# First weight loads of a GNN and mixture-of-experts layer: up matrices of experts 0 to 2 in two transfers in place of three, asked for at other moments

## What is computed

```python
q, k, v = x @ wq.T, x @ wk.T, x @ wv.T                # 1024 x 1024 float32 each
q2, k2, v2 = q @ wiq.T, k @ wik.T, v @ wiv.T
gnn = softmax(q2 k2' / 8 + mask) v2 @ wo.T            # by head
mix = ln(h + attn(h @ mq, h @ mk, h @ mv) @ mo)       # linear attention
...
xe = (x1_norm * score_e)                              # rows scaled by the gate's score of expert e
h = square(relu(bf16(xe) @ bf16(w_up[e]).T))          # w_up: 8 x 1408 x 1024, given in float32
routed += bf16(h) @ bf16(w_down[e]).T                 # w_down: 8 x 1024 x 1408, given in float32
shared = square(relu(x1_norm @ shared_up.T)) @ shared_down.T   # float32
```

## Time and profile before

| what | us |
|---|---|
| median of 3 runs | 359.33 |
| the 3 runs | 359.3, 361.91, 359.33 |
| the profiled execution: its time | 357.42 |
| the profiled execution: its span | 356.1 |
| PE busy in the span | 307.5 |
| DVE, ACT, POOL busy | 111.4, 59.0, 34.2 |

### The profile page before, as it was taken

How to read it: one execution, slowest core, us unless ns; L and a number is a source line. 1 busy time by engine, 2 the same in 40 slices (tenths; PEclk the granted TensorE clock), 3 DMA queues, 4 the chain that set the end, 5 groups by cost and what they waited for, 6 DMA issues and landing times.

```text
span 356.1 us, 3105 instructions
## 1 busy us (share of the span) xinstructions
PE 307.5 (86%) x1236; PEld 149.9 (42%) x1236; DVE 111.4 (31%) x246; ACT 59.0 (17%) x113; POOL 34.2 (10%) x62
## 2 busy tenths in 40 slices
PE   4999998998999999999959998899998893473674
PEld 4344444333343343433324565543455661241343
DVE  6619436400143439200732312210222330101112
ACT  1410000010003010300020033300223440111131
POOL 0511010110110110211110001000000040000000
PEclk9999999999999999999989999999999996876889
DMA  7999999999999999999999999999999999999997
GB/s 296 387 356 311 395 342 309 353 347 320 431 309 377 393 276 429 265 420 329 307 367 309 211 431 336 218 223 210 225 212 213 225 209 225 213 213 212 209 215 157
DMA packets 8968, 104.90 MB, mean 295 GB/s; under 512 B 1120, under 2 KB 1592, under 8 KB 2812
## 3 DMA queue, kind: packets, MB, share of 16 engines
q0 software_dynamic: 7776, 97.52, 95.0%
q1 hardware_dynamic: 880, 7.05, 5.0%
q10 hardware_dynamic: 300, 0.16, 0.2%
HBM read 150.48 MB, written 0.39 MB: 424 GB/s over the span
## 4 chain that ended last, share of the span: by engine, by line
PE 66%; DMA 26%; DVE 3%; ACT 2%; issue 1%; another core or an unknown queue 1%
PE bank L844 32%; DMA stage<-in_expert_up 14%; PE bank L997 9%; PE bank L1018 9%; PE bank L978 6%; PE bank L1058 5%; DMA ring<-in_mat_wik 4%; DMA ring<-in_mat_mv 4%; DMA ring<-in_mat_wo 4%; PE bank L968 1%; PE bank L815 1%; ACT hbuf L451 1%; PE bank L852 1%; ACT xn L445 1%
## 5 line engine op out<-in xcount | busy, mean ns | idle before, releaser
L844 PE MATMUL bank<-ring,xnt 128*96 128x512 f32 x224 | 99.4, 600 | 0.9 <-ACT xnt L381 0.6
L844 PEld LDWEIGHTS bank<-ring,xnt 128*96 128x96 f32 x224 | 36.3, 165 | 58.8 <-issue 57.7
L1018 PE MATMUL bank<-stage,hbuf 128*96 128x512 bf16 (+5 forms) x242 | 44.0, 341 | 18.1 <-DMA stage<-in_expert_down 14.7
L997 PE MATMUL bank<-stage,hbuf 128*96 128x512 bf16 (+1 forms) x192 | 44.2, 384 | 10.1 <-DMA stage<-in_expert_up 9.6
L844 PE MATMUL bank<-ring,stage 128*96 128x512 f32 x96 | 42.2, 594 | 1.2 <-DMA ring<-in_mat_wik 1.2
L1018 PEld LDWEIGHTS bank<-stage,hbuf 128*96 128x96 bf16 x242 | 26.7, 129 | 33.6 <-issue 18.8
L997 PEld LDWEIGHTS bank<-stage,hbuf 128*96 128x96 bf16 x192 | 24.0, 130 | 26.7 <-issue 14.7
L790 DVE TENSOR_TENSOR acc<-acc_t,acc 96x512 f32<-96x512 bf16 (+5 forms) x22 | 11.9, 542 | 56.2 <-ACT acc_t L470 55.9
L844 PEld LDWEIGHTS bank<-ring,stage 128*96 128x96 f32 x96 | 15.3, 163 | 24.3 <-issue 22.9
L445 ACT ACTIVATE xn<-bank 96x512 bf16<-96x512 f32 (+2 forms) x26 | 14.6, 560 | 65.1 <-PE bank L997 58.8
L777 DVE TENSOR_TENSOR xn<-xn 96x512 bf16<-96x512 bf16 (+1 forms) x24 | 9.6, 399 | 44.6 <-ACT xn L445 44.6
(11 more groups left out here) (161 smaller groups left out, 192.5 us busy)
## 6 DMA issues: line engine op xcount, KB each, us to landing
stage<-in_expert_up POOLq DMA_DIRECT2D x4, 2816.0 KB, 31.0
stage<-in_expert_down POOLq DMA_DIRECT2D x4, 2816.0 KB, 37.5
stage<-in_expert_down POOLq DMA_DIRECT2D x6, 1408.0 KB, 16.6
stage<-in_expert_up POOLq DMA_DIRECT2D x6, 1024.0 KB, 13.8
ring<-in_shared_down POOLq DMA_DIRECT2D x2, 2816.0 KB, 13.0
ring<-in_mat_wq SPq DMA_DIRECT2D x2, 2048.0 KB, 11.1
ring<-in_mat_wv POOLq DMA_DIRECT2D x2, 2048.0 KB, 12.0
ring<-in_mat_wiq POOLq DMA_DIRECT2D x2, 2048.0 KB, 13.7
```

The lines of the kernel that those rows point to most:

```text
L844: ins = mm(bank[BANKS[m] + h][0:N, :], tiles(src)[:, k, :], w[:, k, :], start=(k == 0), stop=(k == KT - 1))
L997: ins = mm(bank[4 + j][0:N, 0:c1 - c0], tiles(xe)[:, k, :], w[:, k, :], start=(k == 0), stop=(k == KT - 1))
L1018: ins = mm(bank[j % 4][0:N, 0:c1 - c0], tiles(e_h)[:, t, :], w[:, t, :], start=(t == 0), stop=(t == TT - 1))
```

## The change

The up matrices of experts 0, 1 and 2 are loaded in two transfers (tiles 0 to 6, tiles 6 to 11) in place of three (0 to 4, 4 to 8, 8 to 11). That makes 12 first loads in place of 15. FIRST_AT has new moments for all of them, down halves too, and FIRST_LANDED, the index of the load that waits for the scratch memory and the counts that TensorE waits for follow.

```diff
 FIRST_LOADS = [(e, m, x0, x1) for e in range(3) for m, x0, x1 in
-               [(0, 0, 4), (0, 4, 8), (0, 8, 11), (1, 0, HALF * TT), (1, HALF * TT, D * TT)]]
-FIRST_AT = [0, 3, 6, 9, 13, 16, 21, 24, 29, 32, 37, 39, 42, 44, 44]
+               [(0, 0, 6), (0, 6, 11), (1, 0, HALF * TT), (1, HALF * TT, D * TT)]]
+FIRST_AT = [0, 4, 6, 12, 16, 21, 26, 30, 37, 38, 44, 44]
...
-                        if n == 10:
+                        if n == 8:
                             pool.wait_ge(pv_psum, 2)
                             pool.wait_ge(mvec_t_psum, 2)
                         load(*FIRST_LOADS[n], FIRST_LANDED[n])
...
-            expert(0, 0, HALVES, 32, None, None, None, None)
+            expert(0, 0, HALVES, 16, None, None, None, None)
```

More of the change, by code:

```diff
@@ L195, in gps_layer @@
         part_landed = [sem(f"part_landed{j}") for j in range(len(FINE))]
-        FIRST_LANDED = [up_landed[0], up_landed[0], part_landed[4], part_landed[2], part_landed[3],
-                        up_landed[1], up_landed[1], part_landed[0], down_landed[1], part_landed[1],
-                        up_landed[2], up_landed[2], up_landed[2], down_landed[2], down_landed[2]]
+        FIRST_LANDED = [up_landed[0], part_landed[4], part_landed[2], part_landed[3],
+                        up_landed[1], part_landed[0], down_landed[1], part_landed[1],
+                        up_landed[2], up_landed[2], down_landed[2], down_landed[2]]
         out_landed = sem("out_landed")
@@ L1046, in _ @@
                 pe.wait_ge(part_landed[j], 16)
-            expert(0, 0, HALVES, 32, None, None, None, None)
+            expert(0, 0, HALVES, 16, None, None, None, None)
             for j in (0, 1):
                 pe.wait_ge(part_landed[j], 16)
-            expert(1, 1, HALVES, 32, 16, None, (out_taken, 1, 2), None)
+            expert(1, 1, HALVES, 16, 16, None, (out_taken, 1, 2), None)
             for j, (c0, c1) in enumerate(HALVES):
@@ L1063, in _ @@
                 at, turn = i * ROUND, i * 16
-                expert(i * 3 + 2, 2, HALVES, turn + 48, turn + 32, None, (added, at + 6, at + 6), None)
-                expert(i * 3 + 3, 0, HALVES, turn + 48, turn + 16, None,
+                expert(i * 3 + 2, 2, HALVES, turn + 32, turn + 32, None, (added, at + 6, at + 6), None)
+                expert(i * 3 + 3, 0, HALVES, turn + 32, turn + 16, None,
                        (out_taken, at + 5, at + 6), None)
-                expert(i * 3 + 4, 1, FINE, turn + 48, turn + 32, turn + 16,
+                expert(i * 3 + 4, 1, FINE, turn + 32, turn + 32, turn + 16,
                        (out_taken, at + 7, at + 8), at + 8)
```

## The result

The changed kernel takes 361.91 us (median of 20 runs, 360.06 to 365.14) where the kernel before takes 358.81 us in the same comparison: ratio 1.0086, 95% interval 1.0066 to 1.0105, so 3.1 us (2.4 to 3.8) slower. The forecast was 359.4 with a range up to 361.5. It stood on 359.33, the median of 3 runs of before, and was a change of +0.1 us; +3.1 us were measured. The change is slower, by more than the range allowed, though still under 1%.

A forecast was written before the change was run, and what follows sets the result against it. The DMA transfer queue was taken as the bound throughout. A saving of 0.5 us for three transfers fewer and a 0.6 us gap at expert 3's up load gave +0.1 us: 359.33 to 359.4 us, range 357.6 to 361.5.

The forecast's parts named there:

- only if the queue runs dry: Whole kernel: the end moves only if the DMA queue runs dry somewhere or a transfer has its own cost.
- wiv 1: Front load: lands at 98.0 in place of 95.6, making PE wait 2.3 us, the largest new wait.
- mq 1: Front load: lands at 114.1 in place of 110.5, making PE wait 0.6 us.
- wiq 0: Front load: lands at 59.7 behind a down half, making PE wait 1.2 us in place of the wait for wik.
- PE's delay at the experts: PE comes to the experts 2.4 us late, which by itself costs nothing; late requests count.
- wk 0: First load on SP's queue, beside POOL's six-tile load: its share stays the same, cost 0 with 1.7 us of cover.
- the gap ahead of expert 3's up matrix: The late request, called the tight one, leaves a queue gap of 0 to 1.3 us, 0.6 taken.
- shared down's two requests: Before the experts: they wait for PE's shared up blocks; no cost was put on them.
- saving of 0.5 us for three transfers fewer: Up loads of experts 0 to 2: 0.17 us fixed cost each, gaining 0.5 us, bounds 0 and 1.0.
- Rival 1: PE's clock falls in the new wiv 1 wait; gap up to 2.4 us, time 361.2 us; chance 0.13.
- Rival 3: A transfer's start isn't hidden, so three fewer save up to 9.6 us: 349.7 us; chance 0.02.
- Rival 2: PE so late that the queue runs dry for good, deciding from 4.7 us of delay: 363.4 us; chance 0.04.

The follow-up runs named there:

- e8: Changed kernel, with shared down in three parts asked for early and the first four tiles of expert 3's up matrix asked for early: 358.49 us, ratio 1.0007.
- e5: Kernel before, with only the first four tiles of expert 3's up matrix asked for early: 357.81 us, ratio 0.9987.
- e10: Kernel before, with 5 idle matmuls ahead of expert 0: 359.27 us, ratio 1.0029.
- e2: Changed kernel's two transfers of six and five tiles, at moments that put no more tiles ahead of the front's halves than the kernel before: 358.78 us, ratio 1.0004.
- e11: Kernel before, with 22 idle matmuls ahead of expert 0: 362.21 us, ratio 1.0106.
- e9: Changed kernel, with shared down in three parts asked for early and expert 3's up matrix asked for as in the changed kernel: 359.93 us, ratio 1.0045.
- e3: Kernel before, with 11 idle matmuls ahead of expert 0 and no transfer moved or resized: 361.82 us, ratio 1.0095.
- e4: Changed kernel, with the first four tiles of expert 3's up matrix asked for early: 360.94 us, ratio 1.0044.
- e1: Changed kernel, with the first six tiles as two transfers of three asked for together, same order: 361.98 us, ratio 1.0085 against the kernel before.
- e7: Kernel before, with 11 idle matmuls behind the shared expert's first up block, so shared down's requests are late too: 361.30 us, ratio 1.0074.

## Why the prediction was wrong

- **The bound was right, the way to lose time only in part.** The end is set by the DMA queue: e8 shows it, with PE as late as in the changed kernel and no loss. But "only if the queue runs dry" was too narrow. In the changed kernel's profile the engines keep a share of 0.95 at the place that loses 2.6 us, and what grows is the time of the first rows, and of one engine.
- **The order on the clock was right.** wiv 1 was forecast to land at 98.0 and landed at 81.85 + 16.4 = 98.2; mq 1 at 114.1, measured 114.1; wiq 0 at 59.7, measured 60.0. PE's delay at the experts was forecast as 2.4 us and is 2.36, and expert 3's request was put at 217.6 and came at 217.55. The wait for wiq was 0.4 us in place of 1.2, because PE was 1.1 us behind already: its first 32 matmuls took 16.50 us in place of 15.40. That can't be put down to the change: they took 16.3 in e5 and 17.0 in e10, whose front is the one of before. Since the landing of wiv 1 sets the delay anyway, it changed nothing behind.
- **A term put at nothing that is not nothing, without effect here: wk 0.** The prediction said that "its share is the same". Beside a first load of six tiles wk 0 takes 25.5 us from its issue in the changed kernel and 26.2 in e2, against 23.0 before. In e2 PE waits 1.4 us for it; in the changed kernel PE came 0.3 us after it.
- **The term that failed: the gap ahead of expert 3's up matrix**, 0 to 1.3 us with 0.6 taken. In the profiled execution it is 2.6 us. I had read a start of at most 3.2 us from the windows at 218.1, set it against the moment when the last engines get free, and called the difference the gap. The start is only 1.1 to 1.5 us (e11), so by that subtraction alone nothing would have been lost. What the sum left out is that a load that comes late costs more than its wait: its first rows take 2.5 us in place of 1.7, and the landing is that of the last of 16 engines. Why the first rows are slow and one engine falls behind is not shown.
- **How much queue is enough.** At expert 3's up matrix, in one execution each, 4.7 and 4.0 us left lost nothing (before, e2), 3.7 lost 0.6 (e10), 2.8 lost 2.3 (e9), 2.6 lost 2.6 (the changed kernel), 2.0 lost 1.6 (e3), 0.2 lost 2.8 (e11). That 2.0 lost less than 2.6 lies in the single engine: it is 1.7 us behind the 15 others in the changed kernel and in e9, and 0.8 in e3. The mean of the 16 engines falls behind steadily, by my reading of the small packets' times, 0.9 us at 2.6 left, 1.7 at 2.0 and 3.2 at 0.2.
- **The place that was put at nothing: shared down's two requests.** I named them as waiting for PE and called expert 3's "the tight one". With PE's delay they come with 3.9 to 4 us of queue left, and the square of e4, e8 and e9 puts half of the 3.1 us on them. In the changed kernel's profiled execution they lose only 0.2 us. They lose much where PE is later than my sum had it, as in e1's execution (2.8 left, 3.3 lost) and in e7 (2.7 left, 2.7 lost). How often the changed kernel has such executions is not shown.
- **The saving of 0.5 us for three transfers fewer** is not there. e1 against the changed kernel and e2 against before both give under 0.2 us, within some 0.8 us. The fit took it from landings rounded to 0.1 us.
- **The rivals.** Rival 1 is not refuted. In the changed kernel's profile PE's clock did not fall in the wait for wiv (the 16 matmuls behind it take 7.08 us, and the shared block takes 8.80 as before), but in e1's, with the same order and nearly the same wait, it did. e8's profile has a fall to 0.57 in 61 to 65, behind its wait for wiq, and loses nothing by it, since its requests come early. So a fall adds to PE's delay in some executions, and what it costs is decided at the requests. Rival 3 fell with e1 and e2: the moments moved the time, the number of transfers did not. Rival 2's mechanism, a dry queue because PE is late, is nearest to the right one, but I had it decide from a delay of 4.7 us, and it costs 3 us at 2.4.
- **The rule on fixed cost.** The Trainium skill ("DMA: Bandwidth & Descriptors", "Anatomy of one DMA") gives 2.0 us plus the bytes at 436 GB/s. It has its place where the queue is empty: the estimate from it is 15.2 us for expert 3's up matrix, and e11 measured 16.3. The 1 MiB that I set beside it is missed by the three-tile loads only in what they write (0.79 MB); they read 1.57.

Left open: why the first rows of a late load are slow, why one engine falls behind, and how the loss of an average execution is shared out. Executions of one kernel differ by 2 to 5 us, and not all of that is late requests: in e4, e7 and e10 one later landing comes 1.1 us late with over 15 us of queue left.

## What to carry to other kernels

Where one queue sets the end, ask of every request how much of the queue is left when it is made, and list all of them behind a delay, not the shortest alone. In this kernel 4 us and more lost nothing as long as nothing had been lost ahead, and under 3 us cost 1.6 to 3.3 us. Take the delay with its spread: the same wait left PE 1.7 us later where the clock fell behind it. An engine with over 20 us of waits later on isn't free to be late if its progress is what frees the buffers. The cheap cure is to ask for the first part of a buffer as soon as that part is used; at both places together it took away all of a 3 us loss without a change to the order.

## What the runs showed of the hardware

- A GpSimd transfer of 128 x 11264 elements (float32 read, bfloat16 written) takes 13.3 us from landing to landing behind another one, and 16.3 us from its request when the queue is empty (e11). Its first rows start 1.1 to 1.5 us after the request and take 2.5 us each in place of 1.7. With 2 to 3 us of queue left it was 16.9 (e3), 18.4 (e9) and 18.5 us (the changed kernel) from the request.
- Such a transfer has landed when the last of 16 DMA engines is done. In the changed kernel 15 were done by 234.1 and the last let the landing wait until 236.05.
- Behind a wait of PE of 2.4 us the granted clock was 1.00 in one execution (16 matmuls in 7.08 us) and 0.57 over 4 us in another (8.77 us).
- Splitting these loads further cost nothing that can be measured while the queue is full: 15 first loads against 12 in the same order gave ratios of 1.0085 and 1.0086.
